# Scattering routed feed-forward outputs: two fp32r products on a split operand against one plain fp32 product

## The reference

```python
# q_idx: for each batch and each of g=4 groups the NQ=128 tokens chosen by top_k
o = jnp.einsum('bgne,gde->bgnd', o, w_out)          # (b=2, g=4, 128, d=128)
o = o * q_scores
flat_idx = q_idx.reshape(b, g * NQ)
flat_o = o.reshape(b, g * NQ, d)
summed = jnp.zeros_like(x).at[b2, flat_idx].add(flat_o)
counts = jnp.zeros((b, n), x.dtype).at[b2, flat_idx].add(1.0)[..., None]
meaned = summed / jnp.clip(counts, 1e-05)
return jnp.where(counts > 0, meaned, null_token)
```

## Time and profile before

| | |
|---|---|
| timed runs, median (lowest to highest of 3) | 840.73 us (840.03 to 842.59) |
| profiled execution, span | 884.5 us |
| PE busy | 671.1 us, 76% of the span |
| PE weight loads busy | 499.8 us, 57% |
| DVE busy | 485.9 us, 55% |
| ACT busy | 438.0 us, 50% |
| POOL busy | 332.6 us, 38% |
| mean granted TensorE clock | 0.885 of full speed |

### The profile page before, as it was taken

The page is one execution under the profiler, slowest core; times in us unless marked ns, Lnnn a source line. Parts: engine busy times, 40 slices in busy tenths (PEclk is TensorE's granted clock), DMA queues, the critical chain, the costliest instruction groups (busy, mean ns, idle before and its releaser), DMA issues.

```text
span 884.5 us, 13419 instructions
## 1 busy us (share of the span) xinstructions
PE 671.1 (76%) x4694; PEld 499.8 (57%) x4694; DVE 485.9 (55%) x1449; ACT 438.0 (50%) x835; POOL 332.6 (38%) x393
## 2 busy tenths in 40 slices
PE   4389798379999993287996498988649657988980
PEld 2266785122222242266896487878537646877880
DVE  7878748931111129877748144445457843454563
ACT  6374324579999978264316333334324642333440
POOL 1390322213223323371303545655340073655443
PEclk8589999769999998599998599999859878999996
DMA  9100000567000000000002745556220056655554
GB/s 340 47 0 1 1 1 1 185 237 248 2 1 1 1 1 4 0 1 1 1 1 54 243 147 175 171 181 195 83 76 1 2 149 214 200 157 159 185 151 151
DMA packets 35687, 83.36 MB, mean 94 GB/s; under 512 B 5024, under 2 KB 19872, under 8 KB 35104
## 3 DMA queue, kind: packets, MB, share of 16 engines
q1 hardware_dynamic: 30496, 71.87, 25.0%
q0 software_dynamic: 5120, 10.58, 4.0%
HBM read 65.62 MB, written 16.81 MB: 93 GB/s over the span
## 4 chain that ended last, share of the span: by engine, by line
PE 55%; DVE 21%; ACT 10%; issue 8%; DMA 3%; POOL 1%; another core or an unknown queue 0%; SPq 0%; DVEq 0%; ACTq 0%
PE ps L1921 17%; PE ps L1932 7%; PE ps L1833 6%; PE ps L1602 3%; PE ps L1728 3%; ACT arena L1414 3%; PE ps L1816 3%; DVE arena L708 2%; PE ps L1700 2%; DVE arena L706 2%; PE ps L1709 1%; ACT Xn L1239 1%; DVE stats L613 1%; DVE arena L785 1%; DMA arena<-xs,wq 1%
## 5 line engine op out<-in xcount | busy, mean ns | idle before, releaser
L1921 PE MATMUL ps<-arena 128*128 128x256 f32 (+1 forms) x768 | 163.7, 367 | 34.3 <-issue 31.1
L1921 PEld LDWEIGHTS ps<-arena 128*128 128x128 f32 x768 | 134.5, 204 | 54.2 <-issue 34.6
L1469 ACT ACTIVATE arena<-ps,arena 128x256 f32<-128x256 f32 (+1 forms) x192 | 83.6, 439 | 164.2 <-issue 71.0
L958 DVE SCALAR_TENSOR_TENSOR arena<-ps,arena 128x256 f32<-128x256 f32 (+1 forms) x192 | 83.5, 438 | 124.3 <-ACT arena L1469 101.3
L1414 ACT ACTIVATE arena<-ps 128x1024 f32<-128x1024 f32 (+2 forms) x160 | 135.7, 955 | 3.4 <-PE ps L1816 2.2
L586 POOL DMA_INDIRECT yd<-arena,wq x80 | 78.8, 985 | 110.6 <-DVE arena L980 96.5
L550 POOL DMA_INDIRECT arena<-xs,wq x80 | 77.8, 972 | 31.2 <-issue 21.0
L1833 PE MATMUL ps<-arena 128*32 128x512 f32 (+3 forms) x768 | 82.7, 502 | 2.7 <-DVE arena L1191 1.6
L538 POOL TENSOR_SCALAR_AFFINE_SELECT arena<-arena 128x512 f32<-128x512 f32 x64 | 40.8, 637 | 111.0 <-ACT arena L1414 111.0
L1932 PE MATMUL ps<-arena 128*128 128x128 f32 x640 | 79.5, 275 | 2.0 <-DVE arena L980 2.0
L1932 PEld LDWEIGHTS ps<-arena 128*128 128x128 f32 x640 | 75.2, 192 | 2.5 <-issue 2.4
(11 more groups left out here) (295 smaller groups left out, 1272.0 us busy)
## 6 DMA issues: line engine op xcount, KB each, us to landing
arena<-in_wall SPq DMA_DIRECT2D x48, 836.0 KB
arena<-scr_q SPq DMA_DIRECT2D x8, 512.0 KB, 6.6
arena<-scr_k SPq DMA_DIRECT2D x8, 512.0 KB, 8.3
arena<-yd SPq DMA_DIRECT2D x8, 512.0 KB, 5.4
xs<-Xn SPq DMA_DIRECT2D x8, 260.0 KB, 5.0
scr_q<-arena SPq DMA_DIRECT2D x4, 384.0 KB, 4.1
scr_k<-arena SPq DMA_DIRECT2D x4, 384.0 KB, 3.9
arena<-xs,wq POOLq DMA_INDIRECT x80
```

Of the source, the lines that this page charges most:

```text
L958: nc.vector.scalar_tensor_tensor(out=hT[:, j % 2, f, 0:rows], in0=ps[:, 3 + k % 3, 0:rows], scalar=raw[:, slot, EW_BB + f:EW_BB + f + 1], ...
L1469: nc.scalar.activation(sl[:, k % 3, 0:rows], ps[:, k % 3, 0:rows], ACT.Silu, bias=raw[:, slot, EW_BA + f:EW_BA + f + 1]).then_inc(sem("sil ...
L1921: ins = mm(ps[:, bank, 0:rows], raw[:, slot, w + P * f:w + P * (f + 1)], xTt[:, j % 2, 0:rows], start=True, stop=True)
```

## The change

`evac_out` now writes two tiles instead of one. `O[0]` (`o_high`) gets the scaled block as fp32r, that is rounded; `O[1]` (`o_low`) gets the scaled block minus `o_high`, also as fp32r, by a second DVE instruction that reads PSUM once more. Between the two stands a wait for the first to have landed (`link`), and the semaphore `O` is raised by the second. `ST` is the same memory, now typed fp32r (0 and 1 are exact in it). The scatter runs two products for each block, one with `o_high` and one with `o_low`, both fp32r and both into the same PSUM region. The two tiles lie in the free part of the region of `S`, behind `ST`, and the region of the old `O` is gone, so the tiles carved behind it begin 1,056 words earlier.

```diff
-                   ... ("oT", 2 * FE), ("O", B * G * 132),
+                   ... ("oT", 2 * FE), 
...
-        ST = v["S"][:, 0:B * G * T].rearrange("p (b g t) -> p b g t", b=B, g=G)
+        ST = rounded("ST", carve.at["S"], [P, B, G, T])
...
-        O = v["O"].rearrange("p (b g d) -> p b g d", b=B, g=G)
+        O = [rounded(n, carve.at["S"] + B * G * (T + D * k), [P, B, G, D]) for k, n in enumerate(("o_high", "o_low"))]
...
                     dve.wait_ge(*at("outp", i, n + 1))
-                    nc.vector.tensor_scalar(O[:, b, g, 0:D], ps[:, 7, D * (n % 2):D * (n % 2) + D],
-                                            qs[:, 32 + n:33 + n], None, ALU.mult).then_inc(sem("O", i), 1)
+                    link(nc.vector.tensor_scalar(O[0][:, b, g, :], ps[:, 7, D * (n % 2):D * (n % 2) + D],
+                                                 qs[:, 32 + n:33 + n], None, ALU.mult))
+                    nc.vector.scalar_tensor_tensor(out=O[1][:, b, g, :], in0=ps[:, 7, D * (n % 2):D * (n % 2) + D],
+                                                   scalar=qs[:, 32 + n:33 + n], in1=O[0][:, b, g, :].bitcast(F32),
+                                                   op0=ALU.mult, op1=ALU.subtract).then_inc(sem("O", i), 1)
...
-                            ins = mm(ps[:, 4 * b + j // 2, 256 * (j % 2):256 * (j % 2) + D],
-                                     ST[:, b, g, P * j:P * (j + 1)], O[:, b, g, 0:D], start=(g == 0), stop=(g == G - 1))
+                            for part in range(2):
+                                ins = mm(ps[:, 4 * b + j // 2, 256 * (j % 2):256 * (j % 2) + D],
+                                         ST[:, b, g, P * j:P * (j + 1)], O[part][:, b, g, :],
+                                         start=(g == 0 and part == 0), stop=(g == G - 1 and part == 1))
```

More of the change, by code:

```diff
@@ L220, in build @@
                    ("kT", G * ET * B * 2 * KEYS), ("V", G * B * FE), ("Pm", 2 * FH * KEYS),
-                   ("PT", 2 * ET * NQ), ("PTn", 3 * NQ), ("nvT", G * ET * FH), ("nvw", G * D), ("nl", 2 * FH), ("oT", 2 * FE), ("O", B * G * 132),
+                   ("PT", 2 * ET * NQ), ("PTn", 3 * NQ), ("nvT", G * ET * FH), ("nvw", G * D), ("nl", 2 * FH), ("oT", 2 * FE),
                    ("L", HALF), ("LW", HALF), ("GT", HALF), ("EQ", HALF), ("CE", HALF),
```

## The result

The changed kernel took **877.79 us** (median of 4 runs, 873.71 to 879.77) against 841.55 us (4 runs, 840.03 to 842.59): ratio 1.0398, 95% interval 1.0368 to 1.0427. That is 36.2 us slower, where 1.6 us were forecast.

A forecast was written before the change was run, and what follows sets the result against it. TensorE was taken to bound the kernel, with weight loads pacing the scatter. Products at 0 us plus the second DVE instruction at +1.5 us gave 842.3 us, +0.18%, no change; range about 840 to 846 us.

The forecast's parts named there:

- The price of an fp32r product of 128 columns: In the scatter: each costs one weight load, 0.1117 us, so 14.3 us per scatter as before, 0 us change.
- the last line of the prediction: Scatter: the prediction fails above all if an fp32r product of 128 columns doesn't go by its load.
- narrow fp32r products are dear: Rival, scatter: 128-column fp32r products cost 0.223 us each, 28.6 us per scatter, 871 us in all; chance 0.10.
- The second DVE instruction: L842 delays each block 0.37 us, hidden in full rounds, exposed twice per feed-forward before last outp and scatter: +1.5 us.
- The step that failed: In the sum: terms come from full-clock stretches with direct handovers, so 0 + 1.5 us carry over one to one.
- The clock rival: Fewer columns per load lower TensorE's clock within the scatter, +5 to +14 us each, 852 to 870 us; chance 0.03.
- The argument against the rival, the 8-column products of the earlier trace: Behind the scatter, 8-column products keep their 0.1113 us pitch over 1.9 us, but they are few.
- The rival of the falling load floor: In the scatter, products cost their columns only, 0.058 us each, 7.4 us per scatter, 828 us in all; chance 0.04.
- The range: Whole kernel: bounds 841.8 and 845.2 us, opened by the spread of earlier timed runs to about 840 to 846 us.

The follow-up runs named there:

- e7: Changed kernel with four plain fp32 identity products added ahead of each of the two waits before the scatter; 844.34 us against 842.61, ratio 1.0025.
- e6: Changed kernel with one DVE instruction per block as before, both fp32r products using the rounded part; 842.21 us against 842.61, ratio 0.9998.
- the second trace of before: The kernel before, unchanged, run again for a second profile; 842.89 us, ratio 1.0007, span 839.0 us.
- e1: Kernel before plus the second DVE instruction and its wait, second tile unused, scatter still plain fp32; 848.07 us against 842.44, ratio 1.0055.
- v1: Changed kernel with both output parts and the 0/1 matrix in fp16 instead of fp32r; 836.87 us against 843.56, ratio 0.9923.
- e3: Changed kernel with both parts side by side in one 256-column fp32r product per block, DVE adding both halves; 848.38 us against 842.61, ratio 1.0054.
- e5: Kernel before plus second DVE instruction and wait, each plain scatter product cut into two of 64 columns; 927.96 us (profiled) and 871.49 us.
- e4: Changed kernel with each fp32r scatter product streaming its block twice, 256 columns instead of 128; 848.99 us against 842.44, ratio 1.0088.

## Why the prediction was wrong

- **The price of an fp32r product of 128 columns: right.** 0.11 us in the first products of the changed kernel, 14.25 us per scatter in e7 and 14.5 us in e6 against 14.3 forecast. So the last line of the prediction, that it fails above all if such a product doesn't go by its load, named the wrong danger: the product did. The rival *narrow fp32r products are dear* was wrong, although its time (871 us) lies near the measured one. A half clock and a product of twice the price give about the same 0.21 to 0.22 us; only the granted clock and the first products, at 0.11 us, tell them apart.
- **The second DVE instruction: right as a length.** It lasts 0.351 us (0.344 taken), twice on the chain per feed-forward, at the places named. In the full rounds it was hidden with 0.1 us to spare: L842 ends at 107.85 us and L794 starts at 107.95, in rows of the changed kernel:

```profile
107.50 0.35 DVE L842 SCALAR_TENSOR_TENSOR o_low<-ps,arena,o_high 128x128 fp32r<-128x128 f32 x1
107.95 0.70 DVE L794 TENSOR_REDUCE arena<-ps 128x8 f32<-128x520 f32 x1
```

- **The step that failed** is the one in the sum: "All terms come from stretches in which TensorE was granted its full clock and in which the engines hand over directly, so I carry them over one to one". The 0.37 us of DVE were priced as 0.37 us of delay. They were also idle time of TensorE, next to idle time that was there already, and that lowered the clock. The last column of the timeline has it, in the second trace of before and in the changed kernel:

```profile
124.07 1.13 PE L1709 MATMUL ps<-wout,arena 128*128 128x128 f32 x8 [0.54 <-DVE arena L840]
...
126.06 1.16 PE L1728 MATMUL ps<-arena 128*128 128x128 f32 x8 [0.44 <-DVE arena L840]
```

```profile
123.95 1.13 PE L1712 MATMUL ps<-wout,arena 128*128 128x128 f32 x8 [0.92 <-DVE o_low L842]
...
126.32 0.33 PE L1732 MATMUL ps<-o_high,ST 128*128 128x128 f32 x1 [0.83 <-DVE o_low L842]
```

  The delay itself was right: 0.92 - 0.54 and 0.83 - 0.44 are 0.38 and 0.39 us. What the sum put at nothing is the clock of the scatter behind it: 26.9 and 27.1 us where it had 14.3 each, 24.8 us more than before, and the low clock behind them. The terms were taken from rows at full clock, while the edit changed what the clock depends on.
- **The clock rival was there, with 0.03 and with the wrong cause.** It had the narrow stream lower the clock within the scatter. e6 shows two scatters in which it doesn't: 14.5 us of it at 1.00 in each. Its price, up to 14 us per scatter or 870 us, was about right for the scatters and left out what a low clock costs behind them. And it looked for the danger in one edit at a time; e1 has the waits alone (+5.6 us), e6 the narrow products alone (0), and the change, which has both, +36 us. The argument against the rival, the 8-column products of the earlier trace rows, was true and beside the point: they too kept a clock that was up. Their like in the changed kernel, behind the second scatter, ran with it down (3.21 us for the 16 against 1.77).
- **The rival of the falling load floor: wrong, as forecast.** Two passes did not halve the scatter, 14.25 us in e7. v1 shows what does: fp16 operands.
- **The range was narrower than its own working.** 841.8 and 845.2 us, opened by 0.7 us below and 1.9 us above, are 841.1 and 847.1, not 840 and 846. The measured 877.8 lies far outside either.

The Trainium skill ("TensorE: Matmul & The Clock Gate", section "Why this matters for your kernels") warns of idle time between bursts of products. The runs agree in direction: e7 differs from the changed kernel by filled waits alone, and its clock stays up. The idle pieces here were 0.92 and 0.83 us, shorter than the gaps that the section warns of, and they were enough.

What stays open: why the clock fell in the changed kernel each time (by the trace of one execution, and by the times of all four, none of which is below 873 us) but not in the first scatter of v1 and the second of e3 after the same waits, and perhaps in only one of two executions of e5. Whether it can fall without the added waits is open too, as the one long execution of e6 has no trace. Where exactly the waits begin to matter was not searched for. That the narrow stream keeps the clock down rests on the two scatters of the changed kernel and the two of one execution of e5.

## What to carry to other kernels

Before adding a short wait ahead of a dense stretch on TensorE, read the granted clock of that stretch and ask what would happen at the lower level: here such waits cost their length and 1.6 us per scatter where the clock came back (e1), and their length and nearly the whole stretch once more, with low clock behind it, where it didn't. Replacing a plain fp32 product by two fp32r products of the same width saved nothing here, where the weight loads set the pace. What did save was fp16 for both parts: 0.054 us for a product with its load. Where a wait can't be avoided, a few products without use ahead of it can be cheaper than the idle time: sixteen of them saved 33 us (e7).

## What the runs showed of the hardware that I had not expected

- Two stretches of the same 128 products on the same operands: 14.25 us each when the clock was up at the start (e7), 26.9 and 27.1 us when it had fallen, with no return in the 26 us that followed. In both PE is busy all the time.
- After a fall the clock came back within the scatter with 256 columns per fp32r load (e4), plain fp32 with 128 columns (e1), fp16 with 128 columns (v1). Not so with 128 columns per fp32r load (the change) or 64 plain columns per load (e5, one traced execution).
- An fp16 product of 128 columns costs 0.054 us with its load, an fp32r one 0.111 us (the loads of e7). Twice the columns add little to the fp32r one: with 256 the loads stand 0.12 us apart (e3, e4).
- The clock fell while TensorE waited and no product ran, 0.15 us ahead of the first product (e5, first scatter).
